# Attention on one core: VectorE takes the low part of the first projection before it adds the output products to x

## What is computed

```
x = x + attention(layernorm(x))
Q = einsum('btd,hkd->bthk', x, W_Q) + b_Q      # K and V alike
scores = einsum('bqhk,bshk->bhqs', Q, K) / sqrt(64)
out_h = einsum('bhqs,bshk->bqhk', softmax(scores), V)
return einsum('bqhk,hdk->bqd', out_h, W_O) + b_O
```

## Time and profile before

| | |
|---|---|
| median of 3 runs | 1160.9 us (1159.48 to 1166.03) |
| profiled execution, its own time | 1164.99 us |
| its span, first to last instruction | 1163.7 us |
| mean granted TensorE clock | 0.985 of full |
| busy: TensorE, VectorE, ScalarE, GpSimd | 94%, 72%, 53%, 65% |
| a phase of pairs 1 to 14 | some 21 to 25 us, one of 30 |

### The profile page before, as it was taken

The page is one execution under the profiler, slowest core; times in us unless marked ns, Lnnn a source line. Parts: engine busy times, 40 slices in busy tenths (PEclk is TensorE's granted clock), DMA queues, the critical chain, the costliest instruction groups (busy, mean ns, idle before and its releaser), DMA issues.

```text
span 1163.7 us, 19598 instructions
## 1 busy us (share of the span) xinstructions
PE 1096.0 (94%) x7549; PEld 672.9 (58%) x7549; DVE 835.9 (72%) x1223; ACT 619.0 (53%) x867; POOL 761.6 (65%) x393
## 2 busy tenths in 40 slices
PE   5899999999999999999899999978879988899998
PEld 1456566566566565665556656877534434445786
DVE  4757668567577586576686755525799999998987
ACT  3535445445355355454334534545985665856753
POOL 3587869868868788777578980041389897995200
PEclk9999999999999999999899999989899999999999
DMA  6000000000000000000000215367464453451000
GB/s 204 2 1 2 1 1 1 2 1 2 1 2 1 2 1 1 2 1 1 1 1 11 69 39 184 97 179 219 153 207 155 146 163 130 142 163 38 11 10 18
DMA packets 38076, 68.85 MB, mean 59 GB/s; under 512 B 5952, under 2 KB 24128, under 8 KB 37984
## 3 DMA queue, kind: packets, MB, share of 16 engines
q1 hardware_dynamic: 34976, 64.52, 17.6%
q0 software_dynamic: 1024, 2.10, 0.6%
q10 hardware_dynamic: 1984, 0.98, 0.3%
HBM read 61.30 MB, written 6.16 MB: 58 GB/s over the span
## 4 chain that ended last, share of the span: by engine, by line
PE 76%; DVE 8%; issue 7%; POOL 5%; ACT 2%; DMA 2%; SPq 0%; POOLq 0%; DVEq 0%; ACTq 0%
PE psum L621 18%; PE psum L589 15%; PE psum L605 6%; PE psum L593 5%; PE psum L637 5%; PE psum L987 3%; PE psum L893 3%; PE psum L970 3%; PE psum L671 3%; POOL hc L2108 3%; PE psum L685 2%; PE psum L652 2%; PE psum L762 2%; PE psum L751 1%; DVE psum L1788 1%
## 5 line engine op out<-in xcount | busy, mean ns | idle before, releaser
L2020 POOL TENSOR_TENSOR psums<-psums,prob 128x1024 f32<-128x1024 f32 x180 | 427.8, 2376 | 26.7 <-POOL psums L2020 1.3
L1507 DVE TENSOR_REDUCE mx<-psum 128x2 f32<-128x1024 f32 x256 | 301.1, 1225 | 41.4 <-PE psum L605 41.0
L1078 ACT ACTIVATE prob<-psum 128x1024 f32<-128x1024 f32 x256 | 261.7, 1027 | 67.7 <-PE psum L593 42.8
L621 PE MATMUL psum<-prob,V 128*64 128x512 f32 x1024 | 248.9, 601 | 0.0
L2108 POOL TENSOR_TENSOR hc<-hs,cc 128x1024 f32<-128x1024 f32 x64 | 151.7, 2370 | 21.2 <-DVE hs L1795 18.7
L1795 DVE TENSOR_TENSOR_SCAN hs<-dA,psum 128x1024 f32<-128x1024 f32 x64 | 146.3, 2286 | 2.2
L2020 POOL TENSOR_TENSOR psums<-prob 128x1024 f32<-128x1024 f32 x30 | 72.2, 2407 | 115.5 <-ACT prob L1078 115.5
L621 PEld LDWEIGHTS psum<-prob,V 128*64 128x64 f32 x1024 | 67.9, 137 | 101.0 <-issue 97.2
L893 PE MATMUL psum<-hc,ident 128*128 128x512 f32 x256 | 123.3, 605 | 2.5 <-DVE slot_rows_h L1803 1.4
L605 PE MATMUL psum<-k_hi,q_hi 64*128 64x512 f32 x512 | 108.9, 414 | 4.5 <-DVE mx L1507 1.6
L589 PE MATMUL psum<-q_hi,k_hi 64*128 64x512 f32 x512 | 106.8, 404 | 0.0
(11 more groups left out here) (287 smaller groups left out, 1736.3 us busy)
## 6 DMA issues: line engine op xcount, KB each, us to landing
cc<-C_rows SPq DMA_DIRECT2D x64, 512.0 KB, 3.7
kq_wts<-in_e_rows SPq DMA_DIRECT2D x14, 578.0 KB, 4.8
e_wts<-in_e_rows SPq DMA_DIRECT2D x10, 578.0 KB, 4.0
e_w<-in_e_rows SPq DMA_DIRECT2D x6, 578.0 KB, 4.7
slots_in<-e_zero SPq DMA_DIRECT2D x2, 960.0 KB, 8.2
slots_out<-e_y SPq DMA_DIRECT2D x30, 64.0 KB, 2.5
x<-in_x SPq DMA_DIRECT2D x2, 512.0 KB, 4.9
e_w<-in_e_w SPq DMA_DIRECT2D x1, 1024.0 KB, 7.8
```

The source lines that it names most:

```text
L621: ins = pe.matmul(A.O[HALF[s], :], A.V[pair % 2][:, j, s * DH:(s + 1) * DH], A.prob[unit(pair, c, j) % NPB][:, s * CH:(s + 1) * CH], start ...
L1078: act.activation(A.prob[n % NPB][:, :], slots.bank("score", pair, c, j).rearrange("p s n -> p (s n)"), ACT.Exp, scale=float(DH) ** -0.5).t ...
L1507: dve.tensor_reduce(K.A.mx[:, :, t, c], slots.bank("max", pair, t, c), AXX, ALU.max).then_inc(*slots.inc("max", pair, t, c))
L2020: pool.tensor_tensor(total[:, :], (K.A.prob[(n - 1) % NPB] if j == 1 else total)[:, :], K.A.prob[n % NPB][:, :], ALU.add).then_inc(*K.psum ...
```

## The change

VectorE's adds of "out" become a step of their own, "outed". In `phase` this step stands behind the "lo" of the first projection. In the last pair and in the next layer's order it stands directly behind "out", where VectorE's stream stays as it was. TensorE's order is the same everywhere, as are ScalarE's, GpSimd's and SyncE's.

```
-    order += first[:1] + pv[:1] + first[1:] + pv[1:2] + beside[1] + pv[2:3] + second[:1] + pv[3:4] + second[1:] + beside[3] + pv[4:5]
+    order += first[:1] + pv[:1] + first[1:] + [("outed", last, c)] * (last >= 0) + pv[1:2] + beside[1] + pv[2:3] + second[:1] + pv[3:4] + second[1:] + beside[3] + pv[4:5]
...
-        order += [("out", pair - 1, 0), ("out", pair - 1, 1)]
+        order += [("out", pair - 1, 0), ("outed", pair - 1, 0), ("out", pair - 1, 1), ("outed", pair - 1, 1)]
...
         elif kind == "out":
-            plan_slot(K, "dve", step, slot_of(step))
+            plan_slot(K, "dve", step, slot_of(step), now=False)
+        elif kind == "outed":
+            K.slots.plan_empty("out", *k)
...
-             ... "sumhalf": dve_sum_half, "out": dve_out, ...
+             ... "sumhalf": dve_sum_half, "outed": dve_out, ...
```

More of the change, by code:

```diff
@@ L249, in last_phase @@
     if f == 3:
-        order.append(("out", pair, 0))
+        order += [("out", pair, 0), ("outed", pair, 0)]
     return order
@@ L286, in routed_order @@
     s, beside = NSLOT, {3: [("lnrows", 3)], 4: turned(3), 8: [("scatter", 1, q) for q in range(4)] + [("fetch", NSLOT)], 10: [("fetch", NSLOT + 1)], 12: [("fetch", NSLOT + 2)]}
-    order = [("after", "scores"), ("up", 0), ("gelu", 0), ("sumhalf", LAST, 1), ("lnhalf", 3), ("out", LAST, 1), ("up", 1), ("gelu", 1),
+    order = [("after", "scores"), ("up", 0), ("gelu", 0), ("sumhalf", LAST, 1), ("lnhalf", 3), ("out", LAST, 1), ("outed", LAST, 1), ("up", 1), ("gelu", 1),
              ("fetch", 13), ("after", "attention"), ("pad",), ("lnvar", 3), ("lnroot", 3), ("down", 0), ("yrow", 0), ("fetch", 14)]
@@ L1915 @@
 DVE_STEPS = {"lnvar": dve_moments, "lnhalf": dve_half_moments, "lnrows": dve_rows, "bias": dve_bias, "lo": dve_proj, "maxed": dve_max, "pv": dve_late_sums, "cols": dve_cols,
-             "rowed": dve_row, "valued": dve_values, "sumhalf": dve_sum_half, "out": dve_out, "gsum": dve_gate_squares, "gscale": dve_gate_scale, "gdir": dve_gdir, "choose": dve_choose,
+             "rowed": dve_row, "valued": dve_values, "sumhalf": dve_sum_half, "outed": dve_out, "gsum": dve_gate_squares, "gscale": dve_gate_scale, "gdir": dve_gdir, "choose": dve_choose,
              "rate": dve_rate, "count": dve_count, "yrow": dve_yrow, "return": dve_return, "conv": dve_conv, "xpj_take": dve_xpj_take, "xdr": dve_xdr,
```

## The result

The changed kernel takes 1169.21 us (median of 11 runs, 1167.10 to 1171.18), the kernel before 1162.67 us (11 runs, 1159.48 to 1166.03). The ratio is 1.0058 with a 95% interval of 1.0048 to 1.0069, so the change costs about 6.7 us (5.6 to 8.0). The forecast was 4.9 us more, 1165.8 us on the 1160.9 that were then known of the kernel before, within 1161 to 1170.5 us. The time lies in the range and the sign is right.

A forecast was written before the change was run, and what follows sets the result against it. TensorE was taken as the bound; ordinary phases gave 0 and six phases 1.68 + 1.80 + 0.70 + 1.68 - 0.50 - 0.49 = +4.87 us on the median of 1160.9, so 1165.8 us, range 1161 to 1170.5.

The forecast's parts named there:

- load waits are hidden: Ordinary phases: the second projection's weight load waits 0.41 us for k_lo under matmuls in flight, so removing it gives zero.
- The rival that would have made the kernel faster: Weight loads can't run under matmuls in flight, so 24 waits give back 9.5 us: 1156.3 us; chance 4%.
- basic shift of 1.68 us: VectorE idles for k_hi before k_lo and the adds, so whatever it does next comes 1.68 us later.
- slack of 0.56 us: Ordinary phases: adds end at 315.12, q_lo can't start before 315.68, so the delay costs nothing in 20 phases.
- (3, 0): Phase with lnvar between the low parts: no slack before TensorE's values, +1.68 us.
- (8, 1): Phase with lnvar whose statistics wait for the adds directly ahead; TensorE's transpose waits for the low part, +1.80 us.
- (5, 0) and (12, 1): Bias phase, VectorE's 0.95 us idle time absorbing part: +0.70 us; count phase, no idle time: +1.68 us.
- (11, 1) and (12, 0): Phases where logits or total wait for k_lo, which comes sooner: -0.50 and -0.49 us.
- all behind it follows: In (11, 1), e_top starts at 553.39 in place of 553.89 and everything after moves equally: -0.50 us.
- The clock: No new fall counted behind stalls of 0.7 to 2.1 us; one fall -2.8 to +2.8 us, two at worst +5.6.
- priced as a rival: New stalls, in (12, 1) or a 1.7, bring 1.2 GHz: 1168.6 us for one fall, 1171.4 for two; chance 20%.
- same: Whole kernel: outcome within about 0.5% of no change, 1155.1 to 1166.7 us; chance 0.58.

The follow-up runs named there:

- ordinary phases alone: Adds moved only in phases without other VectorE work between the low parts, six phases keeping the old order, against the kernel before: 1162.07 us, ratio 1.0007.
- GpSimd's sums cut: GpSimd's sums of exponentials cut to 8 of 1024 columns from pair 1, against the kernel before: old order of adds 1163.86 us (0.9934), new order 1168.02 us (0.9975).
- four-phase kernel: Adds moved only in (3, 0), (5, 0), (8, 1) and (12, 1), against the kernel before: 1171.74 us, ratio 1.0087.
- steps moved late: Six groups of next-layer steps moved out from between the low parts, against the kernel before: old order of adds 1157.82 us (0.9954), new order 1155.54 us (0.9940).

## Why the prediction was right, and where it wasn't

- **TensorE is the bound and the load waits are hidden: right.** The ordinary phases alone gave 1.0007, and the second projection's matmul stands where it stood. The rival that would have made the kernel faster is refuted: the loads at 313.58 before and 314.15 after run under matmuls of the same rows. The rule of the Trainium skill that I cited for it (page "TensorE: Matmul & The Clock Gate", section "The mechanism" of Part 3) doesn't hold for these loads. The same section also lets a load run ahead of matmuls when it goes to the background weight buffer, which I had left out and which nothing here contradicts.
- **The basic shift of 1.68 us and the slack of 0.56 us: right.** The idle time of VectorE ahead of the adds grew from 0.66 to 2.33 us, and its slack ahead of q_lo is 0.49 after. (3, 0) lost 1.61 and (8, 1) 1.82, for 1.68 and 1.80.
- **(5, 0) and (12, 1): right mechanism, size off.** The terms +0.70 and +1.68 measured +1.48 and +2.47. The missing 0.8 in each is a VectorE instruction lengthened by GpSimd's adds: the bias 2.14 for 1.31, and the count's first step 1.16 for 0.31. With GpSimd's sums cut they are +0.55 and +0.44, the latter because the count's last step is then short too.
- **(11, 1) and (12, 0): the step "all behind it follows" was wrong.** In (11, 1) the forecast's 0.5 us sooner holds up to e_top (5.71 us behind the phase's start for 6.21), in (12, 0) for k_lo (2.84 for 3.36) but no longer for the copy behind alog (6.72 for 6.44). What follows does not simply slide: the instructions are re-timed by GpSimd's adds, -5.15 in place of -0.50 and +3.37 in place of -0.49. Both sizes include a fall of the clock that went away in one phase and appeared in the other. With GpSimd's sums cut, (12, 0) gives -0.58.
- **The clock: half right.** No fall came behind the stalls of 1.34 to 1.77 us in (5, 0), (3, 0) and (8, 1), nor behind the 2.92 us of (12, 1), for which I had forecast 2.1. But in (12, 0) one came behind the 3.03 us that I had not foreseen, so by the prediction's own sign, a slow clock behind a new stall, it is wrong there. In the four-phase kernel one came in (12, 1), which I had priced as a rival. The price of up to 2.8 us fits only the long fall of before, beside which a shorter one made (11, 1) 1.24 us shorter (28.53 for 29.77). A short one cost about half of it: (11, 1) with and without gives 1.57, and (12, 1) 1.42 (26.04 against 24.62). And a stall is not what it takes: with the steps moved late the clock fell in three profiles of (11, 1) without one, and in two others, one of them of a kernel of those three, it didn't. What sets it off stays open.
- **The total: right sign and size, in part by luck.** The forecast of +4.87 was below the measured 6.7 (5.6 to 8.0), and came this near only because the errors of (11, 1) and (12, 0), -4.65 and +3.86, nearly cancel. The forecast of the time, 1165.8, is 3.4 us low, and 1.8 of these come from the kernel before, whose median went from 1160.9 in 3 runs to 1162.67 in 11. The prediction's own bound for a slower kernel was 1166.7, so the outcome is the one to which it had given 0.38, not the 0.58 of "same". The phases of the two profiles give +5.6, with 29.77 us for (11, 1) of before. In the two kernels that leave this phase in its old order and ran beside it (ordinary phases alone, four phases alone) it took 28.53 and 28.40 us, with a shorter stretch at 1.2 GHz. With these the change's phases sum to +6.9, the measured size. How the clock falls in executions without a profile no trace shows, so this last 1.3 us stays argued.

## What to carry to other kernels

Ask of a swap on an in-order engine not only which instruction gets sooner but what the engine will wait for first: here it traded work that was ready for a wait of 2.3 us, free where slack followed and paid in full where it didn't. When an instruction on few elements takes ten times its usual length, find whose instruction ends with it, and treat its length as a function of its place. Small steps of VectorE with both operands in SBUF belong where GpSimd is idle or where nothing waits for them, which here gave 0.5 to 0.6%.

## What the hardware showed that I had not expected

- A VectorE instruction of 64 columns took 0.20 to 0.23 us with GpSimd's sums cut and up to 2.37 us with them, by GpSimd's adds of 2.4 us. Products, a scan, a cast and a TENSOR_SCALAR on SBUF alone were lengthened; the adds with one operand in PSUM (0.34 to 0.35 us), the low parts (0.72 to 0.75) and the maxima (1.22 to 1.23) never were in the two kernels of the case. And GpSimd's add waits in its turn when VectorE has begun first, 3.17 us for 2.36 beside the bias.
- The same phases repeat within 0.05 us between kernels with different work ahead of them (24.62 and 24.62, 28.51 and 28.47), while whole executions of one kernel lie up to 6.6 us apart (1159.48 to 1166.03).
- In the three profiles on the second chip VectorE stood idle for 3.1 to 3.3 us near 630 us with the releaser given as "remote", in (13, 0), and TensorE stood for 1.2 to 2.1 us beside it. The phase took 22.59, 24.11 and 25.69 us there, the last two with a fall of the clock, and 21.04 to 21.10 in all other profiles. I have no cause for it.
- The clock fell in (11, 1) with no stall above 0.47 us in one profile and none above 0.1 us in three, each time 0.9 to 2.3 us behind the last of the thin matmuls of 8 columns (logits). It stayed at 1.00 behind a stall of 2.92 us in the changed kernel's (12, 1) and fell at the end of one of 2.94 in the same phase of the four-phase kernel.
